# A two-layer decoder on one core: loads and turns between the feed-forward, the attention between batches, and the cross-attention

## The chip, the cores and the metric

One core of a Trainium2 chip runs the whole program. The metric is the device time of one execution in microseconds (us); the profile's times are microseconds from the first instruction. The engines are TensorE (PE, its weight loads PEld), VectorE (DVE), ScalarE (ACT), GpSimd (POOL) and SyncE (SP), whose queue here issues most of the DMAs.

## The reference, cut to what matters

The input x is 4 batches x 512 positions x 512 features. Two decoder layers follow each other, and after each of their three parts x is added and normalised:

```python
x = _layernorm(x + _L0_attn_ref(x, ...))          # linear attention
x = _layernorm(x + _L0_xattn_ref(ctx_1024, x, ...))   # selective scan
x = _layernorm(x + _L0_ffn_ref(x, w_fc, w_proj))      # ternary weights
x = _layernorm(x + _L1_attn_ref(x, weight_qkv, weight_proj))
x = _layernorm(x + _L1_xattn_ref(x, ctx_1024, Wq, Wk, Wv, Wo, gq, gk))
x = _layernorm(x + _L1_ffn_ref(x, lut, gate_idx, up_idx, down_idx))
```

`_L1_attn_ref` reads x as (sequence, batch, features): its sequence is the axis of length 4, and each of the 512 positions is a batch entry of its own. So it is a causal attention of 16 heads (4 key heads, width 32) between the 4 batches, at each position separately:

```python
qkv = x.reshape(-1, hidden) @ weight_qkv.T
...
scores = jnp.where(causal, q @ k.T * scale, -inf)     # 4 x 4 for a position and head
attn = softmax(scores) @ v
out = attn @ weight_proj.T
```

`_L1_xattn_ref` has 16 heads of width 128; queries from x and keys from the context are normalised (RMS) before the scores.

## The kernel before

The kernel has five stages, one after the other: the first layer's two attentions together (stage 0 in the code's tables), the first feed-forward (1), the attention between batches (2), the cross-attention (3) and the last feed-forward (4). Each is worked through in four chunks c. In all stages but one a chunk is a batch: 512 positions, in four tiles of 128. In the attention between batches a chunk is 128 positions of all four batches, since it mixes the batches; its four tiles are the batches b. So its first chunk needs rows of every batch, the last one's too.

Every engine has its own program, and semaphores tie them together. x goes from stage to stage through DRAM: `store_chunk` on GpSimd's queue stores the four normalised tiles `xo` of a chunk after the last of them (semaphore `stored`), and `load_chunk` on SP's queue loads a chunk into `xc[:, c % 2]`, one of two homes, as soon as the last reader of that home is done (semaphore `ln_sum`, counted with `T0`) and, at the start of a stage, the store has landed.

In the attention between batches TensorE turns a chunk (`turn2`, L967: 16 transposes of 128x128), ScalarE copies the result to `xT` (`x_turned`, by the helper `bring`, L1257), and TensorE multiplies with `wqkv` (`project2`, by `group`, L694: two tiles for each batch). ScalarE copies them to `qkv`. From there VectorE and GpSimd work in turns: GpSimd multiplies queries and keys (`scores_of`, L2358), VectorE sums, takes the maximum and subtracts (`scores`, L1964 to L1972), ScalarE takes exponentials (`exps`, L1483), VectorE divides and multiplies the first value (`attend`, L1980 to L1990), GpSimd multiplies the others (L2367) and VectorE adds them (L1997). TensorE turns the attended values (`turn_attended`, L984) and multiplies with `wpr` (`out2`, L694). VectorE adds x (`ln_first`, L265), takes the moments (L270, L273), GpSimd the root (L279, L281), and VectorE normalises (L286).

The order on each engine is written out by hand and pipelined over chunks: TensorE turns and projects chunk c + 1 between the output products of chunk c. The weights `wqkv` and `wpr` are loaded by two DMAs in ScalarE's queue (L1461) when the feed-forward's last eviction is due.

The cross-attention begins with a preparation for its first chunk. Context and weights are split into a rounded part and a rest, for faster products of three terms: ScalarE rounds (`round_ctx`, `round_wxk`, `round_wxv`, `round_wxq`, L1576, L1567, L1572, L1562), VectorE subtracts (`ctx_rest`, `wxk_rest`, `wxv_rest`, `wxq_rest`, L2166, L2158, L2162, L2154). TensorE then makes keys and values (L1034), turns x (L1070) and makes queries (L1034). VectorE squares and sums keys (`key_norms`, L2125 to L2130) and subtracts the rounded x (`x3_rest`, L2171).

Of the kernel before, what the change touches and what calls it, by code (L numbers as in the profile page):

```python
# [25 lines left out]
P = 128  # L26
# [59 lines left out]
def build(nc, io, stages=5):  # L86
# [7 lines left out]
    with ExitStack() as ctx:  # L94
# [40 lines left out]
        stage_loaded = [sem(f"stage_loaded{n}") for n in range(5)]  # L135
# [98 lines left out]
        list3(*[("x", 0, k) for k in range(KD)], *[("qkv", 0, b, n) for b in range(B) for n in range(2)])  # L234
# [15 lines left out]
        A0, V0, T0 = ([sum(per[:n]) * B for n in range(6)] for per in (PER_A, PER_V, PER_T))  # L250
        L0 = [16 * n for n in (16, 2, 2, 2, 2)]

        def x_count(n, i):

            return 16 * (n * B // 2 + i + 1)
# [93 lines left out]
        s3w_at = s2.at  # L349
        s3w = Space(nc, s3w_at)  # L350
# [3 lines left out]
        hr = s2("hr", [P, 2, S]); h2 = s2("h2", [P, 2, S])  # L354
        x_hi = s2("x_hi", [P, KD, S], F32R); x_lo = s2("x_lo", [P, KD, S], F32R)
# [4 lines left out]
        tern_n = sem("tern_n"); tern = sem("tern")  # L360
# [4 lines left out]
        wqkv = s3w("wqkv", [P, KD, QKV]); wpr = s3w("wpr", [P, KD, D])  # L365
# [29 lines left out]
        sq = s4("sq", [P, S])  # L395
        k_hi = s4("k_hi", [P, S], F32R); k_lo = s4("k_lo", [P, S], F32R)
        kr = s4("kr", [P, S])
# [14 lines left out]
        x_hi3 = Space(nc, xT_at)("x_hi3", [P, KD, S], F32R); x_lo3 = s4("x_lo3", [P, KD, S], F32R)  # L412
        wxq = s4("wxq", [P, 2, KD, P]); wxq_s = s4("wxq_s", [P, 2, 2, KD, P], F32R)
        wxk = s4("wxk", [P, KC, 4 * XD]); wxk_s = s4("wxk_s", [P, 2, KC, 4 * XD], F32R)
        wxv = s4("wxv", [P, KC, 4 * XD]); wxv_s = s4("wxv_s", [P, 2, KC, 4 * XD], F32R)
        wxq_hi, wxq_lo = wxq_s[:, :, 0, :, :], wxq_s[:, :, 1, :, :]
# [35 lines left out]
        if max(s1.at, s5w.at, s4.at) > SBUF_END or s3.at > s3w_at or s3w.at > early_at or s5.at > oT_end:  # L452
            raise ValueError(f"too much: {s1.at} {s2.at} {s3.at} {s3w.at} {s4.at} {s5.at} {s5w.at}")
# [21 lines left out]
        def _(sp):  # L475
# [6 lines left out]
            def weights(n, dst, src):  # L482
                sp.dma_start(dst[:], src.rearrange("(k p) n -> p k n", p=P)).then_inc(stage_loaded[n], 16)

# [48 lines left out]
            if stages >= 2:  # L533
# [156 lines left out]
        def _(pe):  # L690
# [260 lines left out]
            if stages >= 3:  # L951
# [42 lines left out]
                for b in range(B):  # L994
                    project2(0, b)
# [1482 lines left out]
```

## Time and profile before

| | |
|---|---|
| median of 3 runs | 2836.32 us (2829.55 to 2836.57) |
| profiled execution | 2836.43 us, span 2834.7 us |
| granted TensorE clock, mean | 0.954 |
| busy: PE, DVE, ACT, POOL | 91%, 72%, 43%, 25% |
| feed-forward's last matmul starts | 950.20 us |
| attention between batches, projections start | 968.96 us |
| cross-attention, keys start | 1155.62 us |

The shares of busy time are means over stages of different kinds. What a change between two stages is worth is to be read around the places where the stages meet: which engine is idle there, for how long, and which of them sets the pace once the stage runs. The difference between the profiled execution's time and its span, 1.7 us, lies outside of the span.

### The profile page before, as it was taken

To read this page: it belongs to the slowest core of one execution; us is meant where nothing else is said; L and a number is where in the kernel's file an instruction comes from. 1 tells how busy PE (TensorE), PEld (TensorE's weight loads), DVE (VectorE), ACT (ScalarE), POOL (GpSimd) and SP (SyncE) were. 2 spreads that over 40 slices of the span, in tenths; PEclk is the share of its full clock that TensorE was granted. 3 is DMA by queue.
4 is the path that set the end of the run, shared out by engine and by line. 5 is a ranking of instruction groups with operands and counts; after the bars stand their busy time and mean duration, and the time that the engine had idled before them with its cause. 6 is when DMAs were issued, how large, how long until landed. Compare 5 with 4: busy or idle time off the path is not lost. (4 is left out here: it accounts for less than half of the span.)

```text
span 2834.7 us, 29502 instructions
## 1 busy us (share of the span) xinstructions
PE 2579.2 (91%) x9938; PEld 1707.4 (60%) x9938; DVE 2044.9 (72%) x3585; ACT 1207.1 (43%) x2171; POOL 705.2 (25%) x617
## 2 busy tenths in 40 slices
PE   6998898989789789789899999999999997999997
PEld 2343433434367555566667776777777774588886
DVE  3879999899975377687868897889878895231332
ACT  3453544634433221356554555465645564021111
POOL 1445445456401156211111220111111110000000
PEclk8989999999989899899999999999999998999999
DMA  4111211112311202322323223322323215100000
GB/s 147 52 46 61 67 65 61 53 37 74 113 58 40 87 30 75 119 100 102 130 71 114 77 79 108 123 75 86 105 71 120 82 46 172 60 9 22 31 15 15
DMA packets 81568, 212.47 MB, mean 75 GB/s; under 512 B 8966, under 2 KB 17414, under 8 KB 77324
## 3 DMA queue, kind: packets, MB, share of 16 engines
q1 hardware_dynamic: 72108, 178.25, 19.0%
q0 software_dynamic: 5472, 21.01, 1.9%
q10 hardware_dynamic: 3840, 11.34, 1.1%
q8 instruction: 80, 1.31, 0.2%
q14 instruction: 68, 0.56, 0.1%
HBM read 164.11 MB, written 46.47 MB: 74 GB/s over the span
## 5 line engine op out<-in xcount | busy, mean ns | idle before, releaser
L2327 POOL TENSOR_TENSOR h<-du,Bb 128x1024 f32<-128x1024 f32 x128 | 312.7, 2445 | 242.6 <-DVE h L1785 240.5
L1780 DVE TENSOR_TENSOR_SCAN h<-bank,h 128x512 f32<-128x512 f32 x256 | 300.0, 1208 | 39.7 <-ACT bank L1366 32.2
L1366 ACT ACTIVATE bank<-dt,A 128x512 f32<-128x512 f32 x256 | 175.6, 690 | 317.8 <-DVE h L1780 317.1
L1554 ACT ACTIVATE p<-bank,sm,rq 128x512 f32<-128x512 f32 x256 | 199.1, 778 | 223.6 <-DVE sm L2198 223.6
L2401 POOL TENSOR_TENSOR rq<-rq,mhalf 128x4 f32<-128x4 f32 x64 | 79.4, 1241 | 819.1 <-DVE rq L2142 819.1
L694 PE MATMUL bank<-pT,v 128*128 128x512 f32 x512 | 231.2, 594 | 0.8 <-ACT pT L1257 0.8
L279 POOL TENSOR_SCALAR rstd<-mv 128x1 f32<-128x1 f32 x96 | 29.9, 312 | 788.2 <-DVE mv L273 788.2
L908 PE MATMUL bank<-h,ident 128*128 128x512 f32 x256 | 148.6, 664 | 53.9 <-DVE h L1785 53.5
L2281 DVE TENSOR_TENSOR h<-bank,sg 128x512 f32<-128x512 f32 (+1 forms) x44 | 30.4, 690 | 228.5 <-PE bank L1205 228.5
L1034 PE MATMUL bank<-x_hi,wxq_s 128*128 128x512 f32 x512 | 169.9, 414 | 23.7 <-DVE wxq_s L2154 22.0
L2194 DVE TENSOR_REDUCE sm<-bank 128x1 f32<-128x512 f32 x256 | 175.0, 684 | 7.6 <-PE bank L1034 7.4
L1785 DVE TENSOR_TENSOR h<-h,Cb 128x1024 f32<-128x1024 f32 x128 | 175.3, 1370 | 7.0 <-DVE h L1780 0.5
L1115 PE MATMUL bank<-ident,p 128*128 128x128 f32 x1024 | 145.0, 299 | 23.9 <-DVE q_lo L2146 18.6
L2065 DVE COPY_PREDICATED val<-msk,val 128x516 f32<-128x516 int32 x192 | 144.4, 752 | 29.3 <-DVE val L2058 2.0
L694 PEld LDWEIGHTS bank<-pT,v 128*128 128x128 f32 x512 | 98.0, 192 | 99.5 <-issue 92.4
L1115 PEld LDWEIGHTS bank<-ident,p 128*128 128x128 f32 x1024 | 127.9, 156 | 34.2 <-DVE p L2207 20.5
L1257 ACT ACTIVATE pT<-bank 128x512 f32<-128x512 f32 x256 | 135.0, 601 | 30.8 <-PE bank L1115 30.6
L909 PE MATMUL bank<-h,ident 128*128 128x512 f32 x256 | 140.8, 634 | 0.0
L2207 DVE TENSOR_SCALAR p<-p,sm 128x512 f32<-128x512 f32 x256 | 124.5, 486 | 9.1
L1034 PEld LDWEIGHTS bank<-x_hi,wxq_s 128*128 128x128 f32 x512 | 100.5, 198 | 50.9 <-DVE wxq_s L2154 26.3
L2058 DVE TENSOR_SCALAR val<-msk,lx,le 128x516 uint32<-128x516 uint32 x256 | 128.3, 544 | 2.1
L1681 ACT ACTIVATE sg<-bank 128x512 f32<-128x512 f32 (+1 forms) x44 | 26.2, 595 | 213.2 <-PE bank L1205 213.2
(248 smaller groups left out, 6081.8 us busy)
## 6 DMA issues: line engine op xcount, KB each, us to landing
wxq_s<-wq_dram SPq DMA_DIRECT2D x48, 512.0 KB, 4.0
Bb<-bc_dram SPq DMA_DIRECT2D x32, 512.0 KB, 3.7
Cb<-bc_dram SPq DMA_DIRECT2D x32, 512.0 KB, 3.7
x_dram<-xo POOLq DMA_DIRECT2D x16, 1024.0 KB, 4.9
xc<-x_dram SPq DMA_DIRECT2D x16, 1024.0 KB, 5.3
woh<-in_Wo SPq DMA_DIRECT2D x64, 256.0 KB, 2.7
wxv_s<-wkv_dram SPq DMA_DIRECT2D x12, 1024.0 KB, 4.9
wxk_s<-wkv_dram SPq DMA_DIRECT2D x12, 1024.0 KB, 8.1
```

Source lines behind the costliest of these rows:

```text
L694: m = pe.matmul(dst, l, r, start=(k == 0), stop=(k == len(pairs) - 1))
L908: pe.matmul(bank[4 + et][:, :], ident[:, :], h[:, G % HR, 0, :], start=False, stop=False)
L909: pe.matmul(bank[4 + et][:, :], ident[:, :], h[:, G % HR, 1, :], start=False, stop=(w == NW - 1))\
L1034: m = pe.matmul(dst, l, r, start=(n == 0), stop=(n == len(pairs) - 1))
L1115: m = pe.transpose(d[:, t * P:(t + 1) * P], p4[:, t, k * P:(k + 1) * P], ident[:, :])
L1366: act.activation(bank[2 + n][:, :], dt[:, c % 2, et, :], ACT.Exp, scale=A[:, et, 2 * w + n:2 * w + n + 1]).then_inc(dA_ready, 1)
L1554: act.activation(p4[:, t, :], bank[4 + t][:, :], ACT.Exp, bias=sm4[:, 4 + t:5 + t], scale=rq[:, hh % 2, 1, t:t + 1], accum_out=sm4[:, 8 + ...
L1780: dve.tensor_tensor_scan(h[:, s, n, :], bank[2 + n][:, :], h[:, s, n, :], 0.0, ALU.mult, ALU.add).then_inc(scanned, 1)
L1785: dve.tensor_tensor(h[:, s, :, :], h[:, s, :, :], Cb[:, w % 2, :, :], ALU.mult).then_inc(hC_ready, 1)
L2065: dve.copy_predicated(val[:, s, :], m, val[:, other, :]).then_inc(lut_step, 1)
L2194: dve.tensor_reduce(sm4[:, t:t + 1], bank[4 + t][:, :], AX.X, ALU.max).then_inc(max_ready, 1)
L2327: pool.tensor_tensor(h[:, G % HR, :, :], du[:, et:et + 1, :].to_broadcast([P, 2, S]), Bb[:, w % 2, :, :], ALU.mult).then_inc(dBu_ready, 1)
```

## The change

Four things change.

1. `wqkv` and `wpr` get a place behind the cross-attention's buffers and are loaded by SP's queue during the feed-forward, behind the loads of its first two chunks of x. ScalarE issues no DMA and waits no more for them.
2. In the attention between batches each chunk of x has its own home: chunks 0 and 1 in `xc`, chunks 2 and 3 in `x2`. Of chunk 0, batches 0 to 2 are loaded when batch 2 is stored (`x_first`). Batch 3's part is turned from the tile `xo[:, 0]` in which the norm left it (`turn_last2`, a tile "xb" of its own, copied by `last_turned`), after the projections of the other three. Its part of `xc` is loaded later, for the addition before the norm.
3. At the entry to the cross-attention the first chunk's tiles 0 to 2 are loaded earlier in the same way, and tile 3 is turned from `xo[:, 0]`.
4. The rounding and subtracting of context, key weights and value weights for its first chunk move into the last chunk of the attention before it: on ScalarE behind the fourth exponentials, on VectorE between the third and the fourth norm tile. The rounding of the query weights waits for the last output product, because their split shares its place with `wpr`.

```diff
 @block.sync
-                for c in range(B):
+                for c in range(2):
+                    load_chunk(1, c, c % 2, rows_of)
+                sp.wait_ge(ln_sum, START + T0[1])
+                weights(2, wqkv, io["wqkv"])
+                weights(2, wpr, io["wpr"])
+                for c in range(2, B):
                     load_chunk(1, c, c % 2, rows_of)
             if stages >= 3:
+                sp.wait_ge(ln_sum, START + T0[1] + 4 * (B - 1))
+                sp.wait_ge(stored, STORED0 + 16 * B + 16 * (B - 1))
+                sp.dma_start(xc[:, 0, 0:B - 1, :], parts_of(kept[1], 0, 0, B - 1)).then_inc(x_first, 16)
+                sp.wait_ge(ln_sum, START + T0[2])
                 sp.wait_ge(stored, STORED0 + 32 * B)
-                for c in range(B):
-                    load_chunk(2, c, c % 2, places_of)
+                sp.dma_start(xc[:, 1, :, :], parts_of(kept[1], 1, 0, B)).then_inc(x_loaded[1], 16)
+                sp.dma_start(xc[:, 0, B - 1:B, :], parts_of(kept[1], 0, B - 1, B)).then_inc(x_loaded[0], 16)
+                for c in (2, 3):
+                    sp.dma_start(x2[:, c - 2, :, :], parts_of(kept[1], c, 0, B)).then_inc(x2_loaded, 16)
...
                         if c == 0:
+                            sp.wait_ge(stored, STORED0 + 32 * B + 16 * (B - 1))
+                            sp.wait_ge(ln_sum, START + T0[3] - 2 * 4)
+                            sp.dma_start(xc[:, 0, 0:NT - 1, :], rows_of(kept[2], 0)[:, 0:NT - 1, :]).then_inc(x_first, 16)
                             sp.wait_ge(stored, STORED0 + 48 * B)
-                            load_chunk(3, c, p, rows_of)
+                            sp.dma_start(xc[:, 0, NT - 1:NT, :], rows_of(kept[2], 0)[:, NT - 1:NT, :]).then_inc(x_loaded[0], 16)
                             load_wxk(1)
                             load_wxv(1)
 @block.tensor
                 def turn2(c):
-                    pe.wait_ge(x_loaded[c % 2], START + x_count(2, c // 2))
+                    if c == 0:
+                        pe.wait_ge(x_first, START + 16)
+                    elif c == 1:
+                        pe.wait_ge(x_loaded[1], START + x_count(2, 0))
+                    else:
+                        pe.wait_ge(x2_loaded, START + 32)
...
+                def turn_last2():
+                    pe.wait_ge(ln_out, START + T0[1] + 4 * (B - 1) + 1)
+                    d = bank3("xb", 0)
+                    for k in range(KD):
+                        m = pe.transpose(d[:, k * P:(k + 1) * P], xo[:, 0, k * P:(k + 1) * P], ident[:, :])
+                    m.then_inc(a_full, 1)
...
                 turn2(0)
-                for b in range(B):
+                for b in range(B - 1):
                     project2(0, b)
+                turn_last2()
+                project2(0, B - 1)
+                pe.wait_ge(x_loaded[0], START + x_count(2, 0))
 @block.scalar
                 act.wait_ge(a_full, START + A0[2])
-                for dst, name in ((wqkv, "wqkv"), (wpr, "wpr")):
-                    act.dma_start(dst[:], io[name].rearrange("(k p) n -> p k n", p=P)).then_inc(stage_loaded[2], 16)
-                act.wait_ge(stage_loaded[2], START + L0[2])
...
                     exps(c, 3)
+                    if c == B - 1 and stages >= 4:
+                        act.wait_ge(ctx4_loaded, START + 16)
+                        act.activation(ctx_hi[:, :, :], ctx4[:, :, :], ACT.Copy).then_inc(ctx_rounded, 1)
+                        act.wait_ge(wxk_loaded, START + 16)
+                        act.activation(wxk_hi, wxk[:, :, :], ACT.Copy).then_inc(wxk_rounded, 1)
+                        act.wait_ge(wxv_loaded, START + 16)
+                        act.activation(wxv_hi, wxv[:, :, :], ACT.Copy).then_inc(wxv_rounded, 1)
...
                         if c == 0:
-                            round_ctx(0)
-                            round_wxk(0)
-                            round_wxv(0)
+                            act.wait_ge(v_full, START + V0[3])
                             round_wxq(0)
                             round_wxq(1)
 @block.vector
                         last(2)
                         if c + 1 < B:
                             scores(c + 1, 2)
+                        elif stages >= 4:
+                            dve.wait_ge(ctx_rounded, START + 1)
+                            dve.tensor_tensor(ctx_lo[:, :, :], ctx4[:, :, :], ctx_hi[:, :, :], ALU.subtract).then_inc(ctx_split, 1)
...
                         first(3)
                         last(3)
```

What is marked "..." on VectorE is the same subtraction for `wxk` and `wxv`; the three calls `ctx_rest(0)`, `wxk_rest(0)`, `wxv_rest(0)` at the start of the cross-attention are gone.

## Rows read from the trace of the kernel before

**Rows 1.** Windows: stretch, its us, busy us (x instructions) by engine, clock, DMA.

```profile
core 0: us, PE busy (x) PEld busy (x) DVE busy (x) ACT busy (x) POOL busy (x), PEclk, DMA share, GB/s
950.60:968.96 18.36, 3.65 (x17) 3.28 (x17) 2.60 (x5) 2.39 (x4) 1.71 (x3) 0.58 0.48 171
...
992.16:1030.04 37.88, 37.88 (x129) 21.55 (x128) 28.70 (x55) 8.22 (x20) 24.22 (x22) 1.00 0.00 1
1030.04:1080.00 49.96, 41.09 (x130) 23.68 (x128) 37.51 (x66) 9.41 (x20) 26.39 (x29) 0.90 0.14 49
1080.00:1121.90 41.90, 39.61 (x129) 23.10 (x128) 29.67 (x57) 9.33 (x20) 25.31 (x25) 0.96 0.27 93
1121.90:1149.36 27.46, 19.87 (x49) 8.76 (x47) 19.07 (x33) 6.91 (x12) 15.47 (x16) 0.88 0.10 38
```

**Rows 2.** Waits of TensorE, 930 to 1200: total us, times, longest.

```profile
PE bank L967 <- DMA xc<-x_dram: 11.2, 2, 8.9
```

**Rows 3.** Timeline, 940 to 1016: start, us, engine, line, operation, idle before.

```profile
950.20 0.39 PE L935 MATMUL bank<-q,h_lo 128*128 128x512 f32 x1
...
954.84 0.83 POOL L2301 DMA_DIRECT2D x_dram<-xo  x1 [1.24 <-DVE xo L286]
959.52 0.92 SPq L480 DMA_DIRECT2D xc<-x_dram  x2
964.63 3.65 PE L967 MATMUL bank<-ident,xc 128*128 128x128 f32 x16 [14.04 <-issue]
...
968.96 23.37 PE L694 MATMUL bank<-wqkv,xT 128*128 128x384 f32 x64 [0.69 <-ACT xT L1257]
...
987.20 0.49 ACT L1257 ACTIVATE qkv<-bank 128x384 f32<-128x384 f32 x1 [2.09 <-PE bank L694]
```

**Rows 4.** Timeline: the last additions of each chunk's attended values.

```profile
1013.42 1.74 DVE L1997 TENSOR_TENSOR at<-at,pv 128x512 f32<-128x512 f32 x1 [0.96 <-POOL pv L2367]
...
1056.85 1.74 DVE L1997 TENSOR_TENSOR at<-at,pv 128x512 f32<-128x512 f32 x1 [0.96 <-POOL pv L2367]
...
1098.76 1.75 DVE L1997 TENSOR_TENSOR at<-at,pv 128x512 f32<-128x512 f32 x1 [0.97 <-POOL pv L2367]
...
1140.70 0.69 DVE L1997 TENSOR_TENSOR at<-at,pv 128x512 f32<-128x512 f32 x1 [0.96 <-POOL pv L2367]
```

**Rows 5.** Waits of GpSimd and of VectorE, 1015 to 1142.

```profile
POOL prod L2358 <- ACT qkv L1257: 3.2, 4, 1.2
...
DVE ssum L1980 <- ACT sce L1483: 0.9, 2, 0.5
```

**Rows 6.** Timeline: the store of the feed-forward's third chunk.

```profile
918.02 0.83 POOL L2301 DMA_DIRECT2D x_dram<-xo  x1 [1.26 <-DVE xo L286]
```

**Rows 7.** Timeline: twelve transposes at the cross-attention's start.

```profile
1169.44 1.51 PE L1070 MATMUL bank<-ident,xc 128*128 128x128 f32 x12
```

**Rows 8.** Timeline, 1144 to 1188: the entry to the cross-attention.

```profile
1144.05 1.05 ACT L1567 ACTIVATE wxk_s<-wxk 128x1024 fp32r<-128x1024 f32 x1
...
1147.91 0.55 DVE L286 TENSOR_SCALAR xo<-rsum,mv,rstd 128x512 f32<-128x512 f32 x1 [1.10 <-POOL rstd L281]
...
1149.36 0.69 DVE L265 TENSOR_TENSOR rsum<-bank,xc 128x512 f32<-128x512 f32 x1 [0.90 <-PE bank L694]
...
1152.20 0.55 DVE L286 TENSOR_SCALAR xo<-rsum,mv,rstd 128x512 f32<-128x512 f32 x1 [1.10 <-POOL rstd L281]
...
1154.15 1.22 DVE L2158 TENSOR_TENSOR wxk_s<-wxk,wxk_s 128x1024 fp32r<-128x1024 f32 x1
...
1155.62 1.19 PE L1034 MATMUL bank<-wxk_s,ctx_hi 128*128 128x512 f32 x2 [6.30 <-DVE wxk_s L2158]
...
1165.05 0.69 DVE L2125 TENSOR_TENSOR rsum<-kt 128x512 f32<-128x512 f32 x1
...
1170.76 1.89 DVE L2171 TENSOR_TENSOR x_lo<-bank,x_hi 128x512 fp32r<-128x512 f32 x3 [4.09 <-ACT x_hi L1257]
...
1187.29 1.06 ACT L1572 ACTIVATE wxv_s<-wxv 128x1024 fp32r<-128x1024 f32 x1
```

**Rows 9.** One line's instructions: duration ns min/median/max, first and last start.

```profile
L1990 DVE TENSOR_TENSOR at<-sce,qkv x16: 691/693/5515, 986.9 to 1135.7; 128x512 f32<-128x512 f32 x16
```

More of the change, by code:

```diff
@@ L134, in build @@
         v_full = sem("v_full")
-        stage_loaded = [sem(f"stage_loaded{n}") for n in range(5)]
+        stage_loaded = [None] + [sem(f"stage_loaded{n}") for n in range(1, 4)]
         down_loaded = [sem(f"down_loaded{n}") for n in range(4)]
@@ L232, in list3 @@
                 TILES3[name] = len(TILES3)
-        list3(*[("x", 0, k) for k in range(KD)], *[("qkv", 0, b, n) for b in range(B) for n in range(2)])
+        list3(*[("x", 0, k) for k in range(KD)], *[("qkv", 0, b, n) for b in range(B - 1) for n in range(2)], ("xb", 0),
+              *[("qkv", 0, B - 1, n) for n in range(2)])
         for c in range(B):
@@ L250, in build @@
         A0, V0, T0 = ([sum(per[:n]) * B for n in range(6)] for per in (PER_A, PER_V, PER_T))
+        A0 = [a + (1 if n >= 3 else 0) for n, a in enumerate(A0)]
         L0 = [16 * n for n in (16, 2, 2, 2, 2)]
         def x_count(n, i):
-            return 16 * (n * B // 2 + i + 1)
+            return 16 * (n * B // 2 + i + 1 - (1 if n >= 3 else 0))
         def hold(eng):
@@ L961, in turn2 @@
                 def turn2(c):
[L963 removed]
+                    if c == 0:
[4 more added lines that the diff above has]
+                        pe.wait_ge(x2_loaded, START + 32)
                     for k in range(KD):
                         d = bank3("x", c, k)
[L966 to L967 removed]
+                        for b in range(B if c else B - 1):
+                            m = pe.transpose(d[:, b * P:(b + 1) * P], x_of2(c, b)[:, k * P:(k + 1) * P], ident[:, :])
                         m.then_inc(a_full, 1)
+                def turn_last2():
[4 more added lines that the diff above has]
+                    m.then_inc(a_full, 1)
                 def project2(c, b):
[L972 removed]
+                    if c == 0 and b == B - 1:
+                        ready3("xb", 0)
+                    else:
+                        ready3("x", c, KD - 1)
                     for n in range(2):
@@ L1065, in turn_x @@
                 def turn_x(c, ks):
-                    pe.wait_ge(x_loaded[c % 2], START + x_count(3, c // 2))
+                    if c:
+                        pe.wait_ge(x_loaded[c % 2], START + x_count(3, c // 2))
+                    else:
+                        pe.wait_ge(x_first, START + 32)
+                        pe.wait_ge(ln_out, START + T0[2] + 4 * (B - 1) + 1)
                     for k in ks:
@@ L1495, in _ @@
                 exps(0, 1)
+                last_turned()
                 projected(0, 3)
```

54 lines of the change are left out of this document (32 added, 22 removed).

## The prediction

> **What bounds the kernel now.** I read the stage windows first. TensorE is busy 91% of the span, but not evenly: it is nearly empty from 950.60 to 968.96 us, where the feed-forward ends and the attention between the four batches begins, and it has gaps in that attention's second, third and last stretch and none in its first [rows 1]. The list of TensorE's waits says what ends the large gaps: x loaded from DRAM, 11.2 us in two waits [rows 2]; another, at the entry to cross-attention, is met in part 3. The gap at 950.60 itself is put down to "issue", and the timeline has to be read for it [rows 3]: last matmul of the feed-forward at 950.20, store of the last batch issued at 954.84, load issued at 959.52, when that store had landed, first transpose at 964.63, and the first projection at 968.96. That is a round trip of the data through DRAM which nothing covers.
>
> A gap on TensorE is worth its length only if TensorE sets the pace. So I looked at the chain of VectorE and GpSimd in the attention. Its last step for a chunk is the last addition of the weighted values (L1997, batch 3): it ends at 1015.16, 1058.60, 1100.51 and 1141.39 us [rows 4], so 43.4, 41.9 and 40.9 us per chunk, where TensorE has 37.9 us of work per chunk (the stretch 992.16 to 1030.04, busy throughout [rows 1]). VectorE and GpSimd bound this stage, and TensorE runs ahead of them at its start. In the whole of it (from 1015 on) they wait for TensorE's products only little: GpSimd for the copied projections 3.2 us in four waits, VectorE for ScalarE's exponentials 0.9 us in two (these are queued behind such copies) [rows 5].
>
> **Part 1, start of the attention.** Removed: store, load, 16 transposes and copies after the feed-forward. In their place the load of batches 0 to 2 is issued once batch 2 is stored: that store was issued at 918.02 [rows 6], and by this store's and load's length (954.84 to 964.63, 9.8 us [rows 3]) it is in place by about 928, long before 950.6. The weights come during the feed-forward and are no longer issued from ScalarE, which cost nothing there. After the last matmul (950.20 + 0.4) TensorE does 12 transposes, 1.5 us where the clock is high, and ScalarE copies them as they come [rows 7]; the projection began 0.7 us after the end of the transposes (964.63 + 3.65, then 968.96 [rows 3]). The projections can start at 950.6 + 1.5 + 0.7 = 952.8. They started at 968.96: 16.2 us earlier. Further, the first of them ran at half clock (granted clock 0.58 in the stretch before [rows 1]): the eight tiles took 23.37 us, where a tile takes 2.58 us once it runs (a copy of 0.49 and 2.09 idle before it), so 20.64 for eight [rows 3]: 2.7 us of slow start. TensorE now pauses for under 1 us, so I take 2.6 of them. The copy that starts at 987.20 is the last of the first three batches, and moves by 16.2 + 2.6 = **18.8 us**.
>
> The last batch is turned from the norm's tile, whose norm is followed by three more before the store at 954.84. It costs TensorE a pause of about 1.0 us for the copy, plus 0.45 us of transposes taken off the first 16. Behind it stand the last projection and the first transposes of attended values. The chain does not wait for it: from the copy at 987.69 the chain has work until 1015.16, 27.5 us [rows 3, 4], and the projection of batch 3 is wanted only after three products and two sums of GpSimd. TensorE then waits for the last batch's own load, behind the load of chunk 1 in SP's queue: issue at 959.5, about 5.1 us for the first (959.52 to 964.63), some 2 more for the next; here by 967, wanted at about 975. At no cost, then; were it 10 us later, each further microsecond would count once the slack of TensorE (below) is used up.
>
> **Part 2, homes for chunks 2 and 3.** They remove the two DMA waits (11.2 us) and the slow transposes after them. But the chain is the bound, so only what it waited for TensorE comes back. Without the stall in the stretch of 49.96 us, against the chain's 43.4, TensorE is some 6.6 us further ahead of the chain from then on, and all six waits should go: 3.2 + 0.9 = **4.1 us** [rows 5]. Bounds: 0 (each replaced by the next dependence) and, if TensorE were the bound after all, 12.1 + 4.0 us (stretches of 49.96 and 41.90 against 37.88 [rows 1]). I take 4.1, the row that names the chain's own waits. What is late next is TensorE on the chain: it will stand idle some 2 to 3 us per chunk before the transposes of batch 3's attended values.
>
> **Part 3, entry to cross-attention.** Before, context and weights are split by VectorE only after the last norm (1152.20), in three subtractions of 1.22 us; the second is the one at 1154.15, and TensorE's keys start at 1155.62, after 6.30 us of idleness [rows 8]. Now they stand between the third norm tile (ends 1147.91 + 0.55) and the fourth. The key split ends at 1148.46 + 2 x 1.22 = 1150.9, so keys start at about 1151.1, after the last output projection, which ended just before 1149.36 [rows 8]. Added on ScalarE: three roundings of 1.05 us [rows 8], about 2.9 us together since they overlap slightly, ahead of the copy of the third attended tile. That moves the output projection of batch 2 by 2.9 us, and it is covered by the wait for the chain's last addition, which ends at 1141.39 (TensorE is idle for 7.6 us of the 27.46 us from 1121.90 on [rows 1]). Without that cover it would cost 2.9. Moved later: the fourth norm tile, from 1149.36 to 1148.46 + 3 x 1.22 = 1152.1, by 2.7 us, and with it the store and all that SP has queued behind it: the rest of x, the next key and value weights, indices, splits to store. The first user is the rounding of the next value weights at 1187.29 [rows 8], more than 20 us later; hidden. VectorE itself limits the gain: its last norm takes 3.4 us as before (1149.36 to 1152.20 + 0.55), until 1155.5, some small work and two halves of a split (1.7 us together) until 1157.2, and then four key norms of two instructions of 0.69 us and a short one, 1.6 each, until 1163.6; then it subtracts x, which it began at 1170.76 [rows 8]. By TensorE the gain is 1155.6 - 1151.1 = 4.5 us if the keys start at a low clock as before; by VectorE at most 1170.8 - 1163.6 = 7.2. I take **5.5**, between them. The x of the first chunk was hidden behind keys and values and remains so: 0.
>
> **Sum.** 18.8 + 4.1 + 5.5 = 28.4 us. The profiled execution took 2836.43 us, span 2834.7; that gives a span of 2806.3 and **2808.0 us**. The median of the runs, 2836.32, is the same within 0.1 us, though one run had 2829.55. Everything behind is a chain of data that moves along. Some 0.3% (8.5 us) is about what a measurement of this kernel can tell from no change.
>
> **Rivals.** *TensorE is the bound in the attention.* Then 17.2 (start of the attended transposes: 18.8 less the pause and turning of the last batch) + 12.1 + 4.0 + 7.2 = 40.5 us, 2796. For it: the stalls are real and the first stretch is packed. Against it: the additions' times [rows 4]. *Half the smaller terms.* The chain's waits stay and the keys gain 2 at the second entry, because the added ScalarE and VectorE work lies on the path: 18.8 + 0 + 2 = 20.8, 2815.6. *The round trip survives*: TensorE still waits at the start for a load that is in fact late. Then 4.1 + 5.5 remain and the time is 2826.8. Against it: 22 us between batch 2's landing and its use. *GpSimd blocks VectorE more often, and the kernel is slower.* The multiplication L1990 takes 0.69 us, but once 5.52 [rows 9], with GpSimd's products running beside it. Shifted against each other in chunks 2 and 3, the engines could meet so again: 4.8 us for each. It takes six more to eat 28.4 us and eight more for 2836.4 + 10.2 = 2846.6; there are 16 such multiplications, and chunks 0 and 1 of the chain, which wait for nothing of TensorE, keep their alignment.
> The Trainium skill ("SBUF — State Buffer", section "Who interferes with whom") says that VectorE and GpSimd share one pair of ports as an exclusive lock, held for a whole instruction, and that nothing else contends. The trace's one long instruction is in keeping with that. By it packing the two engines closer, which this change does by removing waits between them, is what would cost here.
>
> **Chances.** Forecast (22 to 33 us gained) 0.62; TensorE the bound 0.13; half the terms 0.15; the round trip survives 0.04, of which half within 0.3%; no effect for another reason 0.03; slower by blocking 0.03. The range holds the forecast and the larger parts of both neighbours: 2796 to 2821. Faster by over 0.3%: 0.92; within: 0.05; slower: 0.03.
>
> **What would show it.** The first projection about 2 us after the feed-forward's last matmul, its first tile in 2.6 us; no wait of L967 for DMA; a chunk still about 40 us in L1997, with TensorE waiting for VectorE before L984; the first keys (L1034 before) within 2 us of the last output projection; VectorE's subtraction of x 5 to 7 us closer to it. The prediction is wrong if chunks take 38 us, if L1990 or L1997 often take over 1.6 us, or if a wait for x_first or x_loaded appears.

## The result, and the profile after

The changed kernel took 2807.12 us (median of 12 runs, 2793.51 to 2817.35), the kernel before 2833.12 us in as many runs beside it (2824.17 to 2839.29). The ratio is 0.9917, with a 95% interval from 0.9899 to 0.9934: 23.5 us less, 19 to 29 by the interval; the two medians themselves are 26.0 apart. The profiled executions have spans of 2808.9 and 2834.7 us, 25.8 apart. The forecast of 2808.0 is met, but not by its own sum: one of its three terms had the wrong sign.

To see that, I cut both profiled executions at places that do the same work in both: the end of the feed-forward's last matmul, the end of the last addition of chunk 0 and of chunk 3 in the attention between batches (L1997, now L2056), and the first subtraction of x in the cross-attention (L2171, now L2237). This is the view of windows, first of the kernel before, cut anew (columns: window, its length, busy time and instructions of PE, PEld, DVE, ACT and POOL, granted clock, DMA share, GB/s):

```profile
950.59:1015.16 64.57, 49.85 (x164) 30.12 (x164) 25.14 (x49) 12.72 (x26) 25.05 (x22) 0.84 0.14 49
1015.16:1141.39 126.23, 108.30 (x338) 60.62 (x337) 93.96 (x170) 24.14 (x54) 73.95 (x74) 0.95 0.17 59
1141.39:1170.76 29.37, 22.28 (x72) 15.45 (x72) 17.70 (x34) 9.78 (x16) 7.67 (x11) 0.71 0.49 180
1170.76:2834.70 1663.94, 1562.27 (x6966) 1180.36 (x6964) 1127.83 (x2454) 747.82 (x1466) 212.41 (x260) 0.97 0.24 79
```

and of the changed kernel:

```profile
952.93:998.79 45.86, 44.31 (x161) 26.40 (x159) 25.17 (x49) 12.46 (x27) 25.03 (x22) 1.00 0.41 143
998.79:1127.48 128.69, 110.12 (x341) 59.78 (x340) 102.16 (x169) 24.89 (x57) 72.42 (x74) 0.93 0.09 31
1127.48:1150.79 23.31, 18.77 (x75) 13.40 (x73) 17.45 (x35) 7.06 (x13) 8.08 (x11) 0.93 0.25 82
1150.79:2808.90 1658.11, 1560.43 (x6966) 1178.32 (x6964) 1128.09 (x2454) 746.32 (x1466) 212.53 (x260) 0.97 0.24 81
```

Subtracting row from row gives the ledger, with the prediction's terms beside it:

```
stretch                                     before    after   change   predicted
start to the end of the feed-forward        950.59   952.93    +2.34       0
to the end of chunk 0                        64.57    45.86   -18.71     -18.8
chunks 1 to 3                               126.23   128.69    +2.46      -4.1
entry to cross-attention                     29.37    23.31    -6.06      -5.5
from there to the end                      1663.94  1658.11    -5.83       0
sum                                         2834.70  2808.90  -25.80     -28.4
```

The stretches of the change give 22.3 us; the first and last rows, whose code the change leaves almost alone, give 3.5 more. What those two are is a question for the experiments.

**The start.** The timeline of the changed kernel around the boundary, which answers to [rows 3]:

```profile
952.77 1.47 PE L998 MATMUL bank<-ident,xc 128*128 128x128 f32 x12
953.36 1.64 ACT L1309 ACTIVATE xT<-bank 128x384 f32<-128x384 f32 x4 [16.48 <-PE bank L998]
955.05 15.75 PE L715 MATMUL bank<-wqkv,xT 128*128 128x384 f32 x48 [0.81 <-ACT xT L1309]
957.17 0.83 POOL L2364 DMA_DIRECT2D x_dram<-xo  x1 [1.24 <-DVE xo L288]
961.94 0.37 SPq L558 DMA_DIRECT2D xc<-x_dram  x1
970.63 0.60 PE L1006 MATMUL bank<-ident,xo 128*128 128x128 f32 x4
970.83 0.49 ACT L1309 ACTIVATE qkv<-bank 128x384 f32<-128x384 f32 x1 [2.09 <-PE bank L715]
```

The twelve transposes follow the last matmul (952.54) at once, the projections 0.81 us after them, and all tiles come 2.58 us apart. The copy at 970.83 is the one that started at 987.20 [rows 3]: 16.37 us earlier, 18.71 against the end of the feed-forward. Of these, 16.25 are the earlier first projection (2.12 us after the feed-forward's end, where it was 18.37), and the other 2.46 the slow start that is gone. The store at 957.17 and the load at 961.94 still follow each other as before, and nothing waits for them now.

**The chain.** The last addition of each chunk, which answers to [rows 4]:

```profile
997.05 1.74 DVE L2056 TENSOR_TENSOR at<-at,pv 128x512 f32<-128x512 f32 x1 [0.96 <-POOL pv L2430]
1040.48 1.74 DVE L2056 TENSOR_TENSOR at<-at,pv 128x512 f32<-128x512 f32 x1 [0.96 <-POOL pv L2430]
1083.71 1.74 DVE L2056 TENSOR_TENSOR at<-at,pv 128x512 f32<-128x512 f32 x1 [0.96 <-POOL pv L2430]
1126.79 0.69 DVE L2056 TENSOR_TENSOR at<-at,pv 128x512 f32<-128x512 f32 x1 [0.96 <-POOL pv L2430]
```

By the ends (start plus duration) chunks 1, 2 and 3 take 43.43, 43.23 and 42.03 us, where they took 43.43, 41.92 and 40.88. TensorE waits for no load in this stage any more, and GpSimd and VectorE no longer for a copy or an exponential of ScalarE [rows 5]. The time is lost elsewhere. The multiplication of batch 2 (L1990 before, now L2049) took over 5 us once before [rows 9], and takes 5.5 us in each of the three chunks now. Here is the first of them, with what GpSimd does beside it:

```profile
1021.22 0.83 POOL L2364 DMA_DIRECT2D x_dram<-xo  x1 [0.88 <-DVE xo L288]
1021.67 5.51 DVE L2049 TENSOR_TENSOR at<-sce,qkv 128x512 f32<-128x512 f32 x1
1022.08 2.11 POOL L2430 TENSOR_TENSOR pv<-sce,qkv 128x512 f32<-128x512 f32 x2
1024.14 2.48 POOL L2421 TENSOR_TENSOR prod<-qkv 128x512 f32<-128x512 f32 x2
1029.38 2.49 POOL L2421 TENSOR_TENSOR prod<-qkv 128x512 f32<-128x512 f32 x2 [2.76 <-DVE sc L2023]
```

The multiplication begins 0.45 us after the start of the store's issue, needs 0.69 us, and ends only when GpSimd has finished four products and pauses. GpSimd then waits 2.76 us for VectorE. In the kernel before, the same place in chunk 2 looks like this:

```profile
1080.70 0.83 POOL L2301 DMA_DIRECT2D x_dram<-xo  x1 [0.88 <-DVE xo L286]
1080.85 0.20 DVE L1980 TENSOR_REDUCE ssum<-sce 128x16 f32<-128x48 f32 x1 [0.45 <-ACT sce L1483]
1081.68 2.55 POOL L2367 TENSOR_TENSOR pv<-sce,qkv 128x512 f32<-128x512 f32 x2
1081.69 1.60 DVE L1990 TENSOR_TENSOR at<-sce,qkv 128x512 f32<-128x512 f32 x1
```

There the exponential came 0.45 us late, one of the waits of [rows 5] that the change removed. It pushed the multiplication past the end of the store's issue (1081.53), and the multiplication waited for one product only.

**The entry.** Timeline of the changed kernel, against [rows 8]:

```profile
1134.00 0.55 DVE L288 TENSOR_SCALAR xo<-rsum,mv,rstd 128x512 f32<-128x512 f32 x1 [1.10 <-POOL rstd L283]
1135.60 1.22 DVE L2096 TENSOR_TENSOR wxk_s<-wxk,wxk_s 128x1024 fp32r<-128x1024 f32 x1
1137.10 1.19 PE L1079 MATMUL bank<-wxk_s,ctx_hi 128*128 128x512 f32 x2 [3.85 <-DVE wxk_s L2096]
1140.71 0.55 DVE L288 TENSOR_SCALAR xo<-rsum,mv,rstd 128x512 f32<-128x512 f32 x1 [1.10 <-POOL rstd L283]
1150.79 1.89 DVE L2237 TENSOR_TENSOR x_lo<-bank,x_hi 128x512 fp32r<-128x512 f32 x3 [1.42 <-ACT x_hi L1309]
```

Keys start 9.6 us after the chain's end (1127.48), where they started 14.2 after it (1141.39 to 1155.62): 4.6 us earlier; the subtraction of x comes 6.06 earlier. The granted clock of this stretch was 0.93, and 0.71 before. The eight matmuls of the output projection that precede the keys took 3.70 us (1129.55 to 1133.25), where they took 6.06 before.

### The profile page after: what moved, and what is told of

It is laid out like the page before. It is cut to its first block and busy times, and to the rows that moved or that the text cites. A ratio compares the mean times of both kernels' runs of the same rounds, so it can differ in the third digit from the quotient of the medians.

```text
span 2808.9 us, 29504 instructions
## 1 busy us (share of the span) xinstructions
PE 2570.2 (91%) x9938; PEld 1698.9 (60%) x9938; DVE 2054.8 (73%) x3585; ACT 1203.3 (43%) x2172; POOL 704.5 (25%) x617
## 5 line engine op out<-in xcount | busy, mean ns | idle before, releaser
L1165 PE MATMUL bank<-ident,p 128*128 128x128 f32 x1024 | 139.7, 291 | 23.5 <-DVE q_lo L2212 18.4
L1165 PEld LDWEIGHTS bank<-ident,p 128*128 128x128 f32 x1024 | 121.9, 151 | 34.4 <-DVE p L2270 20.2
```

Of the source, the lines that this page charges most:

```text
L1165: m = pe.transpose(d[:, t * P:(t + 1) * P], p4[:, t, k * P:(k + 1) * P], ident[:, :])
```

## The experiments

All times are against the kernel before on the same chip: its medians were 2828.69 us (first four kernels), 2828.27 (next four) and 2831.78 (last four). "Three chunks" is the time from the end of chunk 0 to the end of chunk 3.

### 1. The round trip put back

```diff
-                sp.wait_ge(stored, STORED0 + 16 * B + 16 * (B - 1))
-                sp.dma_start(xc[:, 0, 0:B - 1, :], ...).then_inc(x_first, 16)
                 sp.wait_ge(ln_sum, START + T0[2])
                 sp.wait_ge(stored, STORED0 + 32 * B)
+                sp.dma_start(xc[:, 0, 0:B - 1, :], ...).then_inc(x_first, 16)
```

Expected:

> The changed kernel with the load of batches 0 to 2 for the attention's first chunk issued only when the last batch is stored, as before; the last batch's part still comes from the norm's tile. Theory A (the chain starts with the copied projections): first transposes some 12 us later at the low clock, the copy of batch 2's projections 14 to 17 us later, and the time 14 to 17 us longer. Rival (TensorE has slack against the chain, so it absorbs part): the chunks' last additions move by less than the copy, time 5 to 10 us longer.

Measured: 2823.4 us (12 runs), ratio 0.9987 (0.9967 to 1.0008). Its timeline:

```profile
952.20 2.79 PE L997 MATMUL bank<-ident,xc 128*128 128x128 f32 x12 [13.67 <-issue]
```

The gap is back and put down to "issue" again. From the end of the feed-forward (938.53) to the end of chunk 0 it takes 60.79 us, 14.93 more than the changed kernel; three chunks take 128.70, as there. The time bears it out: 0.0070 of the ratio, 20 us, with an uncertainty of some 8. The early load alone is most of the gain. The 3.8 us between 60.79 and the 64.57 of before go with the parts that were not undone: twelve transposes instead of sixteen wait for the load, and the last batch is turned from the norm's tile. No run takes these apart.

This profile also shows why single executions mislead here: its span is 2806.6 us, less than that of the changed kernel, since the feed-forward ended 14.4 us earlier in it, in code that is the same.

### 2. The splits put back behind the last norm

```diff
-                    if c == B - 1 and stages >= 4:
-                        act.activation(ctx_hi[:, :, :], ctx4[:, :, :], ACT.Copy)...
...
+                            round_ctx(0)
+                            round_wxk(0)
+                            round_wxv(0)
...
-                            dve.tensor_tensor(ctx_lo[:, :, :], ctx4[:, :, :], ctx_hi[:, :, :], ALU.subtract)...
...
+                            ctx_rest(0)
+                            wxk_rest(0)
+                            wxv_rest(0)
```

Expected:

> The changed kernel with the rounding and subtracting of context, key weights and value weights back at the start of the cross-attention, as before. Theory A: the subtraction of x for the first queries comes about 6 us later after the last addition of the attention, as it did before (29.4 against 23.3 us): 5 to 7 us slower. Rival: VectorE does the same work in either place and is busy up to the key norms, so that only the order changes: 0 to 2 us slower.

Measured: 2815.07 us (10 runs), ratio 0.9948 (0.9929 to 0.9967).

```profile
1130.96 1.22 DVE L2213 TENSOR_TENSOR wxk_s<-wxk,wxk_s 128x1024 fp32r<-128x1024 f32 x1
1132.44 1.19 PE L1079 MATMUL bank<-wxk_s,ctx_hi 128*128 128x512 f32 x2 [8.12 <-DVE wxk_s L2213]
```

Keys start 13.2 us after the chain's end (1119.20), against 9.6; the entry takes 26.96 us against 23.31: the early splits give 3.65 us. The entry before took 2.4 us more still, at a granted clock of 0.71 where this one has 0.87. The 3.65 is itself uncertain: in the eleven profiles that have the changed entry it took 21.88 us (experiment 1, clock 0.97) to 24.72 (the second kernel of experiment 6, clock 0.86), so against the one with a clock near 0.87 the early splits give 2.2. Either way it is less than the 5 to 7 of the first theory and more than the rival's 0 to 2. Between the ratios lie 0.0031, 9 us with an uncertainty of 7, so the time bears out the direction and not the size.

### 3. The weights issued from ScalarE again

```diff
-                sp.wait_ge(ln_sum, START + T0[1])
-                weights(2, wqkv, io["wqkv"])
-                weights(2, wpr, io["wpr"])
...
+                for dst, name in ((wqkv, "wqkv"), (wpr, "wpr")):
+                    act.dma_start(dst[:], ...).then_inc(stage_loaded[2], 16)
```

Expected:

> Changed kernel, with the attention weights issued again from ScalarE's queue near the end of the feed-forward (as before the change, some 16 us ahead of its last matmul) and not from SP's at 780. Theory A, the early weights bring nothing: the first projections begin 2.1 us after the end of the feed-forward's last matmul, as in the changed kernel, and the time is the same within 0.1%. Rival: the weights, which need 8 to 10 us and more beside the store and load of x, become what the first projection waits for now that the round trip is gone: some 2 to 5 us, and a wait of the projection for a load is shown.

Measured: 2808.41 us, ratio 0.9918 (0.9898 to 0.9939). The weights were issued at 939.10, took 7.7 and 9.9 us to land, and were there by 950; the projections started at 957.84, 2.05 us after the end of the feed-forward at 955.79 (2.12 in the changed kernel). Three chunks 128.75. This part of the change brings nothing and costs nothing.

### 4. x of chunks 2 and 3 loaded late

```diff
                 for c in (2, 3):
+                    sp.wait_ge(ln_sum, START + T0[2] + 4 * (c - 1))
                     sp.dma_start(x2[:, c - 2, :, :], ...)
```

TensorE waits for each of the two loads by itself.

> The changed kernel with chunks 2 and 3 of x loaded as late as before (each load waits for the additions of the chunk two before it); their own homes stay. Theory A (the chain of VectorE and GpSimd sets the pace, TensorE's waits for the loads are slack): TensorE waits about 9 and 2 us for DMA again, GpSimd and VectorE again wait some 4 us in all for copied projections and exponentials, but then their instructions meet as in the kernel before (one multiplication of 5.5 us, two of 1.6, where the changed kernel has three of 5.5), so the last addition of chunk 3 comes 2 to 3 us earlier after the feed-forward than in the changed kernel: time 2 us lower to 1 higher. Theory B (the two DMA waits were worth what they lasted): 12 to 16 us slower than the changed kernel.

Measured: 2805.16 us (6 runs), ratio 0.9922 (0.9900 to 0.9943). TensorE's list of waits (in total, times, longest):

```profile
PE bank L999 <- DMA x<-x_dram: 10.0, 2, 7.5
```

So its stalls are back, and yet three chunks take 128.19 us, 0.5 less than without them. In this form the 11 us of waits that the change removed are worth nothing. The rest of theory A did not come: GpSimd waited for copied projections once, for 0.6 us, and not as before, and three multiplications are long in both kernels (5.53, 5.20, 5.51 us here), where one was to be. I call such a multiplication blocked from here on. The blocks can hide what TensorE's lateness costs. It had to be tried without them.

### 5. GpSimd waits for the multiplication

```diff
                     pool.wait_ge(p3_ready, START + after(c, B, b + 1))
+                    if b == 2:
+                        pool.wait_ge(at_first, START + after(c, B, b + 1))
                     pool.wait_ge(at_added, ...)
```

Expected:

> The changed kernel with one wait more on GpSimd: before its value products for batch 2 it waits until VectorE's first multiplication for that batch is done (0.7 us). Theory A (the 5.5 us multiplications are VectorE held up by GpSimd's instructions, after a store issued on GpSimd a moment before): none lasts over 1.6 us, each of chunks 1 to 3 takes 39 to 41 us instead of 42.0 to 43.4, and the time falls by 7 to 11 us. Rival (the length is a record of time in which the chain would have waited anyway): chunks stay at 42 to 43 us, or grow by the added wait of some 0.5 us each: 0 to 2 us slower.

Measured: 2802.42 us (6 runs), ratio 0.9910 (0.9888 to 0.9932). Timeline of the same place:

```profile
1017.28 0.83 POOL L2364 DMA_DIRECT2D x_dram<-xo  x1 [0.88 <-DVE xo L288]
1017.73 0.69 DVE L2049 TENSOR_TENSOR at<-sce,qkv 128x512 f32<-128x512 f32 x1
1018.57 2.09 POOL L2432 TENSOR_TENSOR pv<-sce,qkv 128x512 f32<-128x512 f32 x2 [0.45 <-DVE at L2049]
```

The multiplication starts 0.45 us behind the start of the issue as in the changed kernel, overlaps with it, and takes 0.69 us. None of the 16 takes more. Three chunks take 124.32 us (41.96, 41.76, 40.60): 4.4 less, so a block costs the chain 1.4 to 1.5 us more than the added wait does, and not the 4.8 by which the multiplication is longer. The rest comes back in two ways that the timelines show. With GpSimd paused, the two additions behind the blocked multiplication take 1.49 us together (1027.22 in the changed kernel), and 3.17 here beside GpSimd's products; and GpSimd has its four products done meanwhile. The prediction's rival had put the price of a block at the full length.

### 6. The same wait without the change, and with the late loads

Expected for the kernel before, with the wait of experiment 5:

> Kernel before the change, with one wait added: GpSimd waits for the multiplication of batch 2 before its two products of that batch. Theory A, a blocked multiplication costs the chain about 1.4 us and TensorE's two waits for x (11.2 us) cost it nothing: the three chunks take 124.3 to 125 us instead of 126.2. Theory B, each block costs its whole 4.8 us: 121.4. Theory C, TensorE's waits cost the chain the 4.1 us that the prediction gave them, which the blocks hid: the three chunks take 128.4, that is 124.3 of the changed kernel with the wait and 4.1. It also tells whether what follows the first split of x takes 1664 us, as in the kernel before, or 1656 to 1658, as in all profiles of the changed one: if the former, the change does something behind the boundary as well; if it lies anywhere between, it is where TensorE's clock is granted low.

and for the changed kernel with that wait and the late loads of experiment 4:

> Changed kernel with that wait of GpSimd, and with x of chunks 2 and 3 loaded late again, so that TensorE waits for it twice (10.0 us in the kernel with the late loads alone). With no multiplication blocked on either side, the difference to the kernel with the wait alone is what TensorE's waits cost the chain. Theory A (nothing): the three chunks take 124.3 us within 0.5. Theory C (the prediction's term): 128.4 us.

Measured: 2830.13 us (12 runs), ratio 1.0001 (0.9984 to 1.0017), and 2806.33 us (6 runs), ratio 0.9923 (0.9901 to 0.9944). In the first, three chunks take 41.98 + 43.64 + 40.87 = 126.49 us, although no multiplication is blocked. It is chunk 2 that is longer, by 1.7 us against before, and its timeline has the reason:

```profile
1062.38 2.49 POOL L2358 TENSOR_TENSOR prod<-qkv 128x512 f32<-128x512 f32 x2 [1.66 <-ACT qkv L1257]
1071.41 3.71 POOL L2358 TENSOR_TENSOR prod<-qkv 128x512 f32<-128x512 f32 x3 [1.40 <-ACT qkv L1257]
```

GpSimd waits for copied projections, that is for TensorE. The second kernel shows the same in a smaller size: 41.99 + 42.95 + 40.59 = 125.53. Beside the kernels without the wait:

```
three chunks, us                       as it is     GpSimd waits
before (x of chunks 2 and 3 late)       126.23         126.49
changed                                 128.69         124.32
changed, x of chunks 2 and 3 late       128.19         125.53
```

The right column has no blocks. In it, TensorE's waits for x cost the chain 125.53 - 124.32 = 1.2 us with the late loads as in experiment 4, where nothing else differs. Between the kernel before and the changed one it is 126.49 - 124.32 = 2.2, if all of that difference is put down to these waits. Both expectations miss: it is neither nothing nor 4.1. And in the kernel before the two losses hide each other: its one block, in chunk 1, cost it nothing net (126.23 with it, 126.49 without), because the later chain then waited less for its projections. GpSimd's waits for them in chunk 2, first before, then with the added wait:

```profile
POOL prod L2358 <- ACT qkv L1257: 1.6, 2, 1.2
POOL prod L2358 <- ACT qkv L1257: 3.1, 2, 1.7
```

### 7. The store moved behind the products

```diff
                 values_of(c, 2)
+                if c:
+                    store_chunk(2, c - 1)
                 scores_of(c, 3)
...
-                store_chunk(2, c)
+                if c == B - 1:
+                    store_chunk(2, c)
```

Expected:

> Changed kernel, with GpSimd's store of a chunk of the attention issued after the two products of batch 2 of the next chunk instead of right before them. In the changed kernel the multiplication of batch 2 takes 5.5 us in each of chunks 1 to 3 and begins 0.45 us behind the start of that store's issue. Theory A, the block needs the store's issue right ahead of GpSimd's products: no multiplication takes over 1.6 us, and the three chunks together take about 124.3 us instead of 128.7, as in the kernel in which GpSimd waits. Theory B, the block comes from the products beginning while the multiplication runs, whatever is ahead of them: it stays at 5.5 us, since the products then begin 0.8 us earlier still beside it, and the three chunks stay at 128 to 129 us. Time against the kernel before: about 0.990 by A, 0.992 by B, so the trace decides and not the time.

Measured: 2805.59 us, ratio 0.9912 (0.9884 to 0.9939); three chunks 126.83 us. Timeline:

```profile
1018.96 2.55 POOL L2430 TENSOR_TENSOR pv<-sce,qkv 128x512 f32<-128x512 f32 x2 [1.30 <-DVE sce L2043]
1018.99 1.59 DVE L2049 TENSOR_TENSOR at<-sce,qkv 128x512 f32<-128x512 f32 x1
1020.61 4.75 DVE L2056 TENSOR_TENSOR at<-at,pv 128x512 f32<-128x512 f32 x2
1021.46 0.83 POOL L2364 DMA_DIRECT2D x_dram<-xo  x1
1022.32 2.49 POOL L2421 TENSOR_TENSOR prod<-qkv 128x512 f32<-128x512 f32 x2
```

The multiplication is free of the long block. But of the two additions the second now begins while the store is issued and products follow. By the line's own view, of 1022.2 on:

```profile
L2056 DVE TENSOR_TENSOR at<-at,pv x1: 3203/3203/3203, 1022.2 to 1022.2; 128x512 f32<-128x512 f32 x1
```

It takes 3.20 us, until just after the products pause; no addition took over 1.74 in the changed kernel. The two additions take 4.75 us together, and 3.13 where no issue is beside them (experiment 8). The long wait moved with the store. Theory A's first half holds, its sum does not: I had not asked what would be beside the issue next.

### 8. The stores issued by SP, without and with the wait

```diff
+                            for n in range(B - 1):
+                                sp.wait_ge(ln_out, START + T0[2] + after(n, PER_T[2], PER_T[2]))
+                                sp.dma_start(places_of(kept[2], n), xo[:, :, :]).then_inc(stored2, 16)
...
-                store_chunk(2, c)
+                if c == B - 1:
+                    store_chunk(2, c)
```

A semaphore of their own counts these stores, and those who waited for them wait on it.

> Changed kernel, with the stores of the attention's first three chunks issued by SP, which is idle there, and no longer by GpSimd. With the store moved behind the products of batch 2, the multiplication took 1.6 us in place of 5.5, but the two additions after it took 4.75 us together (1.5 each where nothing is in their way), now with the store's issue and products behind it beside them: the long wait seems to follow the store's issue. Theory A, an instruction of VectorE is held up for several of GpSimd's only where one of these is a store's issue with products right behind it: with no issue on GpSimd the multiplication takes at most 1.6 us, the additions at most 1.75, and a chunk gets shorter than the 42.8 us there by what the additions lost (1.5 us) and by the issue itself, 0.8 us: about 40.5 to 41.5 us, 122 to 125 for three. Theory B, back-to-back products of GpSimd are enough: some instruction still takes over 3 us, and three chunks take over 126 us.

> The same, with GpSimd also waiting for the multiplication of batch 2. If the wait costs no more than it gives once the issue is gone, three chunks take 121.5 to 122.5 us: the 124.3 of the kernel with the wait, less the store's issue three times (0.83 each), as far as that issue stood on GpSimd's path; it overlapped with the multiplication there, and where VectorE's chain set the pace instead the sum stays at 124.3. Against the kernel before about 0.990.

Beside them ran the changed kernel and the kernel of experiment 5 once more:

> The changed kernel once more, on the chip of the two kernels before and the one after it, as the measure for them: 0.992 of the kernel before. Its profile should show the attention as before: 45.9 us from the end of the feed-forward to the end of chunk 0, 128.7 us for three chunks with three multiplications of 5.5 us, and 1656 to 1659 us from the first split of x to the end.

> The changed kernel with GpSimd's wait for the multiplication of batch 2 once more, beside the changed kernel on one chip: by the traces 4.4 us shorter (124.3 in place of 128.7 for three chunks), a ratio to the kernel before lower by 0.0015. The intervals of such ratios have been 0.004 wide, so the times alone are likely to leave it open, and the chunks of the attention decide.

```
kernel                        median     ratio (95%)               three chunks
changed                      2810.71   0.9919 (0.9891 to 0.9947)      128.81
changed, GpSimd waits        2804.69   0.9899 (0.9880 to 0.9918)      124.40
changed, stores by SP        2802.76   0.9899 (0.9881 to 0.9917)      123.15
changed, both                2804.83   0.9898 (0.9878 to 0.9918)      124.35
```

With the stores by SP alone:

```profile
1022.14 0.38 SPq L651 DMA_DIRECT2D x_dram<-xo  x1
1022.83 2.56 POOL L2435 TENSOR_TENSOR pv<-sce,qkv 128x512 f32<-128x512 f32 x2 [1.30 <-DVE sce L2047]
1022.86 1.60 DVE L2053 TENSOR_TENSOR at<-sce,qkv 128x512 f32<-128x512 f32 x1
1024.49 3.13 DVE L2060 TENSOR_TENSOR at<-at,pv 128x512 f32<-128x512 f32 x2
1025.35 5.84 POOL L2426 TENSOR_TENSOR prod<-qkv 128x512 f32<-128x512 f32 x4
```

No multiplication takes over 1.60 us, no addition over 1.74, and three chunks take 123.15 us: the long waits are gone with GpSimd's issue, at 5.5 us less than in the changed kernel and 1.2 less than with the wait. The wait on top of it (124.35) only costs, as the second half of that expectation had it. This is the shortest attention I have. The times point the same way, 8 us less in the median, but the intervals of the four ratios overlap: that a version beats the changed kernel is shown by the traces of the stage and not by the times.

## Why the prediction was right, and where it was not

**Right: the start, 18.8 us, measured 18.71.** Each step is there: transposes right behind the feed-forward, projections 0.81 us after them, 2.46 us of slow start gone where I had 2.6 (granted clock 1.00 in the stretch to the end of chunk 0, 0.84 before), the turn of the last batch without effect on the chain. The projections began 2.1 us after the feed-forward where I had 2.2. Experiment 1 puts back 14.93 of it with one transfer. The early weights bring nothing by themselves, as costed (experiment 3).

**Wrong: the step "all six waits should go: 3.2 + 0.9 = 4.1 us", three chunks 2.46 us longer.** The waits did go, and so the first part of the sentence holds; the gain does not follow from it. Two sizes were off. What TensorE's lateness costs the chain is 1.2 to 2.2 us, by experiment 6, and not the sum of the waits named. And the blocks, which I had made a rival with a chance of 0.03 because it would need six more to eat all of the gain, became three instead of one. The three cost the changed kernel 128.69 - 124.32 = 4.4 us; the one had cost the kernel before nothing net (126.23 - 126.49 = -0.3). So the term is 2.2 gained without blocks, less 4.4, less 0.3: 2.5 lost. The prediction had the right instruction and the right price of its length (4.8), but asked only whether it could turn the sign of the whole and not what two more would do to this term. It also argued that chunks 0 and 1 "keep their alignment": true, and beside the point, since the alignment with the store, which the 0.45 us late exponential had broken in chunks 2 and 3, was what the removed waits restored. Its own sign of being wrong, multiplications of over 1.6 us, did appear: three of sixteen, 5.5 us each, where one of sixteen had been before.

The Trainium skill ("SBUF — State Buffer", section "Who interferes with whom") was cited for a lock that is held for a whole instruction, from which the prediction worked out that packing the two engines closer would cost. The direction agrees. The size agrees where the multiplication starts with a product, 1.60 us: the 0.69 of its own and 0.9 of a product that takes 1.05. It does not where a store's issue is ahead of the products: 5.51 us through four of them. So the one long instruction of the trace before, which the prediction called in keeping with such a lock, was longer than a lock for one instruction gives. There the measurement decides.

**Right, a little small: the entry, 5.5 us, measured 6.06.** Keys came 4.6 us earlier, where I had 4.5; VectorE's end had 7.2 as its bound. The keys did not follow the last output projection within 2 us, as I had it: they came 3.85 us behind, on VectorE's split, because the output projection had ended earlier (5.8 us after the chain's end, 7.9 before). Experiment 2 gives 2.2 to 3.65 to the splits. The rest goes with the granted clock of the stretch, 0.71 before against 0.93 (and 0.87 in experiment 2), as far as profiles of single executions can say; with a clock of 0.97 the same entry took 21.88 us in experiment 1 and 21.89 with the stores by SP. Whether the higher clock comes of the change is not shown.

**The rest, taken as nothing: +2.3 and -5.8.** Until the end of the feed-forward the twelve profiles of the changed kernel and its variants took from 938.53 to 955.79 us, with granted clocks of 0.96 and 0.94 in the two: 17 us for the same instructions of TensorE, and the change's 2.3 is lost in that. Behind the entry all twelve took 1655.8 to 1660.5 us. The kernel before took 1663.9, but with one wait added to it 1660.0, so at least 4 of those 5.8 us are such scatter too. Whether the change gives anything behind the entry is not settled; if so, little. That the median fell within 1 us of the forecast is luck. The forecast took 28.4 us off 2836.4; the medians are 26.0 us apart, from 2833.1. So a gain 2.4 us too large met a start 3.3 us too high, and of the 26.0 the three stretches of the change explain 22.3.

**Of the rivals**, "TensorE is the bound" (2796) is refuted by the chain's periods, which grew while TensorE's waits went. "Half the smaller terms" had the sum nearest to the ledger (20.8 against 22.3), for another reason than its own. "GpSimd blocks VectorE more often" named the right mechanism, at 4.8 us for a block where it cost 1.5, and the kernel did not get slower by it. The round trip did not survive.

## What to carry to other kernels

When the chain that sets the pace is two engines in turns, do not add up its waits for a third: remove the third's lateness in a trial, or count only the length of the period. Before you remove a wait, look at which instruction of the partner the waiting one will then start beside, above all where one of them issues a transfer; a long instruction costs only what the two engines cannot make up afterwards, here 1.5 us of 4.8. And if a queue stands idle, as SP's did here, let it issue the transfers of an engine that is on the chain: that was worth 5.5 us here by the traces, where the early loads of chunks 2 and 3 were worth 2.2 at most, and nothing while the blocks stood.

## What the runs showed of the hardware that I had not expected

An operation of VectorE with two inputs in SBUF that starts while GpSimd issues a store (0.83 us), and is still running when GpSimd's products begin, was held for all products up to GpSimd's next pause: 5.5 us for one of 0.69 (5.2 to 5.5 in 3 of 3 chunks in six profiles, and once in the kernel before), and 3.2 us for an addition when the store was moved. In the fourteen profiles this arrangement occurs 22 times, and each time the operation was held; without it no multiplication of this stage took over 1.6 us and no addition over 1.75. The issue alone doesn't hold it (0.69 us where no product began before it had ended, experiment 5). Products alone don't either. The changed kernel shows that 14 us after the multiplication shown first, without a store:

```profile
1035.52 0.69 DVE L2049 TENSOR_TENSOR at<-sce,qkv 128x512 f32<-128x512 f32 x1
1035.82 2.35 POOL L2430 TENSOR_TENSOR pv<-sce,qkv 128x512 f32<-128x512 f32 x2
```

Here the products start 0.30 us behind the multiplication and it is GpSimd that waits (2.35 us for two, against 2.11 above). In these runs it took both together, and with the stores of the first three chunks on SP's queue it never occurred. Why the two together do this, no run here can tell.
